# Phase 1 of a linear-attention kernel in another order, with part of the weight split moved from VectorE to GpSimd and ScalarE

## The reference

```python
def _linear_attention(x, wq, wk, wv, wo):
    q, k, v = (x @ wq), (x @ wk), (x @ wv)      # 16 heads of 16
    phi_q, phi_k = elu(q) + 1.0, elu(k) + 1.0
    kv = einsum('bshd,bshe->bhde', phi_k, v)
    z = sum(phi_k, axis=1)
    num = einsum('bshd,bhde->bshe', phi_q, kv)
    den = einsum('bshd,bhd->bsh', phi_q, z)[..., None] + 1e-06
    return (num / den).reshape(B, S, D) @ wo

y = layernorm(x)
y = y + _linear_attention(layernorm(y, ln1_g, ln1_b), wq, wk, wv, wo)
h = layernorm(y, ln2_g, ln2_b)
y = y + table[round(h @ w1 / 0.1)] @ w2          # table: gelu on a grid of 0.1
x = x + y
return x + einsum('bsk,nk->bsn', layernorm(x), CB) * (SCB / 127.0) + bias
```

## Time and profile before

| | |
|---|---|
| median of 3 runs | 593.51 us (592.5 to 594.23) |
| the profiled execution | 594.68 us |
| its span from first to last instruction | 592.9 us |
| busy share of the span | PE 93%, PEld 83%, DVE 79%, ACT 65%, POOL 57% |
| phase 1 | from the first chunk to about 181 us of the span |
| mean granted TensorE clock | 0.981 |

### The profile page before, as it was taken

The page is one execution under the profiler, slowest core; times in us unless marked ns, Lnnn a source line. Parts: engine busy times, 40 slices in busy tenths (PEclk is TensorE's granted clock), DMA queues, the critical chain, the costliest instruction groups (busy, mean ns, idle before and its releaser), DMA issues.

```text
span 592.9 us, 11272 instructions
## 1 busy us (share of the span) xinstructions
PE 549.6 (93%) x3610; PEld 490.9 (83%) x3610; DVE 466.2 (79%) x1067; ACT 384.8 (65%) x636; POOL 338.8 (57%) x328
## 2 busy tenths in 40 slices
PE   6899999999996889999999999999999999999893
PEld 6778788888885879889898898988988889898783
DVE  5889998688775487978879788788887888878645
ACT  2475664465565667858669586696865968758650
POOL 3431333324131367786776868768687676776662
PEclk9699998999999999999999999999999999999998
DMA  8321221121001010101101101011010110200001
GB/s 269 122 71 48 94 71 37 35 72 35 16 22 56 1 37 1 71 35 35 71 0 71 39 33 71 0 71 54 16 71 0 71 68 2 71 4 33 36 21 54
DMA packets 11419, 29.47 MB, mean 50 GB/s; under 512 B 2048, under 2 KB 4864, under 8 KB 11392
## 3 DMA queue, kind: packets, MB, share of 16 engines
q1 hardware_dynamic: 9472, 28.32, 13.4%
q10 hardware_dynamic: 1920, 0.79, 0.7%
HBM read 20.71 MB, written 8.39 MB: 49 GB/s over the span
## 4 chain that ended last, share of the span: by engine, by line
DVE 28%; PE 23%; issue 18%; ACT 15%; POOL 13%; DMA 2%; POOLq 1%; ACTq 0%; DVEq 0%; SPq 0%
PE psum L1002 22%; POOL f32r_arena L378 7%; DVE bn_stats L657 4%; ACT grid_index L580 3%; POOL f_arena L371 3%; DVE f_arena L793 3%; DVE f32r_arena L814 3%; ACT f32r_arena L593 3%; DVE f_arena L824 2%; DMA f_arena<-in_L_attn_x_dram 2%; DVE f32r_arena L810 2%; DVE bn_stats_b L657 2%; ACT f_arena L591 2%; ACT f32r_arena L528 2%; DVE f32r_arena L802 2%
## 5 line engine op out<-in xcount | busy, mean ns | idle before, releaser
L1002 PE MATMUL psum<-w_hi,f32r_arena 128*128 128x256 f32 x1280 | 176.9, 284 | 12.3 <-POOL f32r_arena L378 8.6
L1002 PEld LDWEIGHTS psum<-w_hi,f32r_arena 128*128 128x128 f32 x1280 | 164.0, 189 | 22.9 <-issue 16.9
L1002 PE MATMUL psum<-f32r_arena,w_hi 128*128 128x512 f32 x512 | 139.9, 403 | 1.5 <-issue 1.0
L378 POOL TENSOR_TENSOR f32r_arena<-f_arena,f32r_arena 128x512 fp32r<-128x512 f32 x64 | 85.9, 1342 | 94.6 <-ACT f32r_arena L593 54.1
L580 ACT ACTIVATE grid_index<-psum,w_bias_in_steps 128x512 int8<-128x512 f32 x128 | 86.7, 677 | 64.2 <-PE psum L1002 64.2
L1002 PEld LDWEIGHTS psum<-f32r_arena,w_hi 128*128 128x128 f32 x512 | 88.0, 188 | 19.9 <-ACT grid_index L580 5.8
L591 ACT ACTIVATE f_arena<-grid_index 128x512 f32<-128x512 int8 x128 | 80.9, 632 | 24.6 <-POOL f32r_arena L378 14.3
L593 ACT ACTIVATE f32r_arena<-grid_index 128x512 fp32r<-128x512 int8 x128 | 79.3, 619 | 0.0
L1002 PE MATMUL psum<-f32r_arena 128*128 128x256 f32 (+1 forms) x384 | 71.6, 336 | 2.0 <-DVE f32r_arena L696 2.0
L1002 PEld LDWEIGHTS psum<-f32r_arena 128*128 128x128 f32 x384 | 59.2, 195 | 8.4 <-issue 2.2
L802 DVE TENSOR_TENSOR f32r_arena<-f_arena,f32r_arena 128x512 fp32r<-128x512 f32 x64 | 63.2, 988 | 2.1 <-ACT f32r_arena L593 1.8
(11 more groups left out here) (116 smaller groups left out, 916.2 us busy)
## 6 DMA issues: line engine op xcount, KB each, us to landing
f_arena<-in_L_attn_x_dram SPq DMA_DIRECT2D x32, 512.0 KB, 3.3
out_dram<-f_arena SPq DMA_DIRECT2D x15, 512.0 KB, 2.7
f_arena<-in_L_attn_w_dram SPq DMA_DIRECT2D x2, 1024.0 KB, 12.6
out_dram<-f_arena SPq DMA_DIRECT2D x2, 256.0 KB, 3.3
phi_q<-in_L_attn_wk_dram ACTq DMA_DIRECT2D x1, 256.0 KB, 4.7
phi_q<-in_L_attn_wq_dram SPq DMA_DIRECT2D x1, 256.0 KB, 4.9
phi_q<-in_L_ffn_CB_dram SPq DMA_DIRECT2D x1, 256.0 KB, 7.0
phi_q<-in_L_attn_wo_dram SPq DMA_DIRECT2D x1, 256.0 KB, 7.5
```

What stands on the lines that cost most here:

```text
L378: nc.gpsimd.tensor_tensor(t_lo[m % SLOTS], tf[m % 2], t_hi[m % SLOTS].bitcast(F32), ALU.subtract).then_inc(s["t_lo_p"], 1)
L1002: return nc.tensor.matmul(out_, lhs, rhs, start=start, stop=stop, skip_group_check=True)
```

## The change

DVE makes the `bn_stats` in two halves around `phi_key` 0, takes `bn_aggr` behind `phi_key` 1, and then `high1`, `low1` and `phi_query`. PE makes both key pairs before `turn1`, and in chunk 8 the first `gather` comes before `project_bias`. ACT takes both K halves before `gain1`. The wide weights are split in 8 slices of 576 columns, one in each of the first 8 chunks: ACT copies a slice behind `q_relus`, POOL subtracts in the next chunk ahead of `power1`, and ACT takes the sum of absolute values in place of the maximum. In chunk 8 the test of wo moves behind `norm1`. The number of weight columns is the same.

```diff
-    SLICES = PAIRS // 2
+    SLICES = PER_SEQ
     SLICE = W2ND // SLICES
...
@@ gpsimd
+            def weight_rest(n, c):
+                g.wait_ge(s["w_hi_done"], n + 1)
+                g.wait_ge(s["n1_ready"], c + 2)
+                nc.gpsimd.tensor_tensor(w_lo[:, split_cols(n)], w_raw[:, split_cols(n)], w_hi[:, split_cols(n)].bitcast(F32),
+                                        ALU.subtract).then_inc(s["w_lo_done"], 1)
...
+                    if past(c, 1) and splits(c - 1):
+                        weight_rest(it * 2 + (p - 1), c)
                     if within(c + 2):
                         power1(c + 2, p)
...
@@ scalar
+            def rest_flag(n):
+                a.wait_ge(s["w_lo_done"], n + 1)
+                wait(a, s["w_flag"], n)
+                act(rest_size[:, :], w_lo[:, split_cols(n)].bitcast(F32), ACT.Abs,
+                    accum_out=flag_cols[:, bass.ds(n + 2, 1)]).then_inc(s["w_flag"], 1)
...
-                if splits(it):
-                    act(w_hi[:, bass.ds(it * SLICE, SLICE)], w_raw[:, bass.ds(it * SLICE, SLICE)], ACT.Copy).then_inc(s["w_hi_done"], 1)
...
                     k_pair(c, 0)
+                    k_pair(c, 1)
                     if within(c + 1):
                         gain1(c + 1)
...
-                    k_pair(c, 1)
                     if past(c, 1):
                         q_relus(c - 1)
+                    if splits(c):
+                        act(w_hi[:, split_cols(c)], w_raw[:, split_cols(c)], ACT.Copy).then_inc(s["w_hi_done"], 1)
+                    if past(c, 1) and splits(c - 1):
+                        rest_flag(it * 2 + (p - 1))
...
@@ vector
                     if within(c + 2):
-                        stats1(c + 2, p, it + 1)
+                        half_sums1(c + 2, p, it + 1, 0)
                     phi_key(c, 0)
-                    if p == 0 and splits(it):
...
-                        ve.tensor_tensor(w_lo[:, cols], w_raw[:, cols], w_hi[:, cols].bitcast(F32),
-                                         ALU.subtract).then_inc(s["w_lo_done"], 1)
-                    if p == 1 and splits(it):
...
-                        ve.tensor_reduce(flag_cols[:, at], w_lo[:, cols].bitcast(F32),
-                                         AX.X, ALU.max, apply_absolute_value=True).then_inc(s["w_flag"], 1)
+                    if within(c + 2):
+                        half_sums1(c + 2, p, it + 1, 1)
+                    phi_key(c, 1)
+                    if within(c + 2):
+                        mean_var(c + 2, bn, mv1[p], "bn1", "mv1_ready")
+                    if is_chunk(c, PER_SEQ + 1):
+                        flag_value(PP, 2, "flag2")
                     if within(c + 1):
                         high1(c + 1, 1 - p)
-                    phi_key(c, 1)
-                    if is_chunk(c, PER_SEQ + 1):
-                        flag_value(PP, 2, "flag2")
+                        low1(c + 1, 1 - p)
                     if past(c, 1):
                         phi_query(c - 1)
-                    if within(c + 1):
-                        low1(c + 1, 1 - p)
...
@@ tensor
                         key_pair(c, p, 0)
+                        key_pair(c, p, 1)
                         if within(c + 1):
                             turn1(c + 1, 1 - p)
...
-                        key_pair(c, p, 1)
+                        gather(c, p, 0)
                         if is_chunk(c, PER_SEQ):
                             pe.wait_ge(s["a1_ready"], c + 2)
                             project_bias(TP)
-                        gather(c, p, 0)
```

More of the change, by code:

```diff
@@ L125, in build @@
         k8 = sb("grid_index", [P, 2, CHUNK], I8)
+        rest_size = sb("weights_rest_size", [P, SLICE])
         h_bias = sb("w1_bias_in_steps", [P, MT])
@@ L216, in tm, with splits, split_cols @@
             return a.rearrange("p (j d) -> p j d", j=TT)
-        def splits(it):
-            return not isinstance(it, int) or it < SLICES
+        def splits(c):
+            return not isinstance(c, int) or c < SLICES
+        def split_cols(c):
+            return bass.ds(c * SLICE, SLICE)
         def half_tm(a, h):
@@ L427, in pair @@
                         power(0, u2, r2, mv2, "mv2_ready", "u2_ready", "pow2")
-            with g.Fori(0, PER_SEQ // 2) as it:
+            pair(0)
+            with g.Fori(1, PER_SEQ // 2) as it:
                 pair(it)
@@ L669, in stats1, with half_sums1 @@
                 stats(c, x1[p], bn, mv1[p], "bn1", "mv1_ready")
+            def half_sums1(c, p, turn, h):
+                if h == 0:
+                    v.wait_ge(x1_loaded[p], 16 * (turn + 1))
+                for j in (2 * h, 2 * h + 1):
+                    i = ve.bn_stats(bn[:, 6 * j:6 * j + 6], tm(x1[p])[:, j])
+                if h == 1:
+                    i.then_inc(s["bn1"], 1)
             def norm1(c, p):
@@ L892, in pair @@
                     if within(c + 2):
-                        stats1(c + 2, p, it + 1)
+                        half_sums1(c + 2, p, it + 1, 0)
                     phi_key(c, 0)
-                    if p == 0 and splits(it):
-                        cols = slice(it * SLICE, it * SLICE + SLICE) if isinstance(it, int) else bass.ds(it * SLICE, SLICE)
-                        v.wait_ge(s["w_hi_done"], it + 1)
-                        ve.tensor_tensor(w_lo[:, cols], w_raw[:, cols], w_hi[:, cols].bitcast(F32),
-                                         ALU.subtract).then_inc(s["w_lo_done"], 1)
-                    if p == 1 and splits(it):
-                        cols = slice(it * SLICE, it * SLICE + SLICE) if isinstance(it, int) else bass.ds(it * SLICE, SLICE)
-                        at = slice(it + 2, it + 3) if isinstance(it, int) else bass.ds(it + 2, 1)
-                        v.wait_ge(s["w_lo_done"], it + 1)
-                        ve.tensor_reduce(flag_cols[:, at], w_lo[:, cols].bitcast(F32),
-                                         AX.X, ALU.max, apply_absolute_value=True).then_inc(s["w_flag"], 1)
+                    if within(c + 2):
[5 more added lines that the diff above has]
+                        flag_value(PP, 2, "flag2")
                     if within(c + 1):
                         high1(c + 1, 1 - p)
-                    phi_key(c, 1)
-                    if is_chunk(c, PER_SEQ + 1):
-                        flag_value(PP, 2, "flag2")
+                        low1(c + 1, 1 - p)
                     if past(c, 1):
                         phi_query(c - 1)
-                    if within(c + 1):
-                        low1(c + 1, 1 - p)
[L915 to L919, removed]
-                        flag_column(2, SLICES + 1, 4 + SLICES)
                     if is_chunk(c, PER_SEQ + 1):
@@ L930, in pair @@
                         norm1(c + 2, p)
+                    if is_chunk(c, PER_SEQ):
+                        v.wait_ge(s["wo_lo_done"], KT)
+                        ve.tensor_reduce(flag_cols[:, 2 + SLICES:3 + SLICES], wo_lo[:, :].bitcast(F32), AX.X, ALU.max,
+                                         apply_absolute_value=True).then_inc(s["wo_flag"], 1)
+                        v.wait_ge(s["wo_flag"], 1)
+                        v.wait_ge(s["w_flag"], SLICES)
+                        flag_column(2, SLICES + 1, 4 + SLICES)
                     if is_chunk(c, PER_SEQ + 5):
```

2 lines of the change are left out of this document (1 added, 1 removed).

## The result

The change made the kernel slower: 598.5 us median of 4 runs (597.55 to 599.34) against 593.17 us, a ratio of 1.0095 with a 95% interval of 1.0071 to 1.0119. I had forecast 593.1 us, with a range from 587.4 to 596.6. The profiled execution took 597.55 us with a span of 595.7 us, 2.8 us more than before; its mean granted clock was 0.973, before the change 0.981.

The account below looks back on a forecast made before the run. Prediction: POOL's late power holds loop chunks at 9.20 us. Chunks 0 to 8 -1.6, chunk 9 -0.6, chunks 9 to 15 +2.6 gave 0.4 us gain off the 593.51 us median: 593.1 us, range 587.4 to 596.6.

Parts of the forecast that it names:

- start, to chunk 2: Chunk 0: the second gather no longer waits for `gain1`, a gain of 0.5 us.
- loop, chunks 2 to 7: Loop chunks: DVE's saved work returns as a 1.55 us wait for POOL's power; 9.20 us per chunk, no gain.
- chunk 8, until PE resumes: Chunk 8: PE resumes 1.6 us later, at 98.8, with chunk 0's gain of 0.5 us included.
- chunk 8, clock: Chunk 8: low clock stays at 6.83 us, costing 3.4 us as before; bound 1.7 us either way.
- chunk 9: Chunk 9: `flag_value` ahead of cast and `low1` makes the block matmuls wait about 0.6 us.
- chunks 10 to 15: Late chunks: 2.6 us gained of PE's 4.6 us of waits for `phi_key` in chunks 9 to 15; ends 0 and 4.6.
- Chunk 8's idle time: Chunk 8: bias matmuls come behind a gather and PE is idle for 2 to 3 us.
- The chain: Loop: from `norm1` through `turn1`, `gain1`, cast, `low1`, `phi_query`, power and shift to scaling, 9.20 us.
- The early power: Loop rival: cast 0.45 us or more after `bn_aggr`, chunk at 8.3 to 8.4 us, 587.7 us; chance 0.32.
- no slipping-in: Loop rival: POOL's L313 gets in only behind `phi_query`, 0.29 us more in nine chunks, 595.7 us; chance 0.12.
- the held port: Loop rival: the power gets in first and keeps the cast out, chain 10.1 us, 598.4 us; chance 0.02.
- table load: ACT rival: the sum of absolute values loads tables, costing 0 to 8 us, middle 597 us; chance 0.02.

Follow-up runs that it names:

- early_bias_first: Changed kernel with `bn_aggr` ahead of `phi_key` 1 and chunk 8's bias matmuls ahead of gather 0: 586.4 us, ratio 0.9868 to before.
- bias_first: Changed kernel with one step undone, chunk 8's bias matmuls ahead of the first gather again: 592.97 us, ratio 0.9988 to before.
- aggr_early: Changed kernel with `bn_aggr` moved ahead of `phi_key` 1: 588.26 us, ratio 0.9888 to before.
- bias_cut: Changed kernel with only 4 of chunk 8's 32 bias matmuls kept: 590.8 us, ratio 0.9953 to before.
- stats_first: Changed kernel with all four `bn_stats` and `bn_aggr` ahead of both `phi_key` again: 593.13 us, ratio 0.9983 to before.
- weights_only: Kernel before with only the weight work moved to POOL and ACT, every order kept: 592.27 us, ratio 0.9982 to before.
- early_bias_ahead: Changed kernel with `bn_aggr` ahead of `phi_key` 1 and the bias matmuls ahead of chunk 8's key pairs: 586.63 us, ratio 0.9868 to before.

## Why the prediction was wrong, and where it held

The terms of the sum, in us of gain, forecast and read from the two traces:

| term | forecast | measured |
|---|---|---|
| start, to chunk 2 | +0.5 | +2.03 |
| loop, chunks 2 to 7 | 0 | +0.25 |
| chunk 8, until PE resumes | -2.1 | -2.97 |
| chunk 8, clock | 0 (1.7 either way) | -3.93 |
| chunk 9 | -0.6 | -0.39 |
| chunks 10 to 15 | +2.6 | +2.25 |
| sum | +0.4 | -2.76 |

**The step that failed is the clock of chunk 8.** I kept the 6.83 us of the earlier trace rows and left half of that open. It became 17.07 us, and the term that stood at nothing cost 3.93 us. The price is borne out by the traces in which PE does the same matmuls, in one order or the other, from where it resumes to gather 0 of chunk 9: 15.31 us with 6.83 us of low clock (before), 15.33 with 6.83 (early_bias_first), 16.95 with 10.24 (bias_first), 18.56 with 13.65 (aggr_early) and 19.24 with 17.07 (changed, 15.06 of them behind the point where PE resumes).

I had read the earlier trace rows as a low clock behind the bias. By the earlier trace rows the bias runs from 97.20 to 102.64, so the clock fell at 98.93, within the bias; in the changed kernel it fell in the idle time, ahead of the bias. The prediction said itself that PE would be idle 2 to 3 us ahead of this place and that the bias matmuls would follow; the mistake was to take the row of before as the value for another sequence of work, and to bound it by that row's own length. The range was narrow by its own terms, too: the two bounds named for it, 1.7 and 2.6 us, give 597.4 us, not 596. The trace of before had two low stretches with different work in them: the bias, and the start, where PE worked with gaps and no bias:

```profile
13.60:23.84 10.24, 6.92 (x30) 5.97 (x29) 8.40 (x27) 6.13 (x10) 4.79 (x11) 0.50 0.68 209
```

A change that puts a gap and the bias next to each other could have been bounded by the sum of the two, 17.07 us, in place of half of one; 10.24 us more at half speed are up to 5.1 us. That the sum is just what was measured is luck: no run shows that such lengths add, and aggr_early, with gap and bias together, had 13.65 us. With the one step undone that brings gap and bias together, the time is 592.97 us. That this is within 0.2 us of the forecast is luck as well, since 10.24 us of low clock stay and PE resumes 1.99 us earlier.

**What the traces leave open.** The sums of the table differ by 3.2 us, the forecast and the median by 5.4. The profiled execution of before is 1.5 us above its median and that of the changed kernel 0.95 us below. That part of the loss lies in executions that were not profiled, and I can't place it. What is on record of them is their mean granted clock: 0.968 to 0.973 in the changed kernel's four, 0.973 to 0.987 in the 31 executions of the kernel before beside bias_first (median 0.981), and in both the longer executions have, on the whole, the lower clocks. That points at the clock, but not at a place in the kernel. Why the stretch of low clock differs in length between executions of one kernel stays open.

**The start** gave more than forecast. The second gather of chunk 0 no longer waits, as I said, but most of the 2.03 us come with the clock: it is low for 6.83 us in place of 10.24 us there. bias_cut is the changed kernel up to chunk 8; there the low stretch was 10.24 us, and `phi_key` 0 of chunk 2 comes at 39.95, which leaves a gain of 0.72 us, near the 0.5 forecast.

**Chunk 8's idle time** was 3.80 us, not 2 to 3, and the loss until PE resumes was 0.9 us larger than forecast. This term is the smaller miss.

**The loop held.** The chain gave 9.20 us; it is 9.10 to 9.20, with L705 waiting 1.53 us (1.55 forecast), L316, L317 and L322 at 0.43, 1.20 and 2.49 us (0.7, 1.2 and above 2.5 forecast). The early power did not come in this order: the cast is ahead of L316 by 0.28 us (49.97 and 50.25), where my sum gave 0.24; aggr_early shows its point, a cast 0.50 us behind `bn_aggr` (0.45 forecast), and its price, a chunk of 8.46 us against 8.3 to 8.4. The rivals of no slipping-in and of the held port did not happen. The page "SBUF — State Buffer" of the Trainium skill, section "Who interferes with whom", would have the second to issue wait for the first in either direction. With DVE first the rows agree: L316 behind the cast. With POOL first they don't: in stats_first the cast took its usual 0.69 us inside a power that ran from 57.86 to 60.00. In weights_only a cast from 50.52 to 51.21 stood in the middle of a power from 50.20 to 51.84, and both took their usual times; in stats_first the cast ran until 59.96, past the 59.50 at which a power of 1.64 us would have ended, and the power ended 0.04 us behind it.

**The rest held**: `weight_rest` took 1.42 us (1.34 to 1.51), hidden; `rest_flag` 0.69 us and a step of 0.20 us for the sum (0.73 to 1.6), and no table load stands beside it. The Trainium skill, page "ScalarE: Activation LUTs", section "Table sets: the hidden batching unit", lists abs among the functions of every set, and the trace agrees.

## What to carry to other kernels

When an operation moves, follow the consumers of its result on the other engines, too: `bn_aggr` moved by one operation decided 0.7 us per chunk, though neither DVE nor POOL had more to do. Treat a low clock as a result of the order of the work around it: here a gap on PE and a run of tiny matmuls went with 13.65 to 17.07 us of low clock together, and with 6.83 to 10.24 us apart, so a move that brings them together needs a bound well above what either cost before. Small PE work that stood in the gap (bias_first) cost 5.5 us less than the same work behind it.

## What the runs showed of the hardware

- The clock stayed at 1.2 GHz for 17.07 us although PE was busy for 15.06 of them; 32 matmuls of one column took 6.83 us of that (4.54 us in early_bias_ahead, 2.50 of them at full speed). With extra matmuls of no use in the gap the median was 6 us lower, though the one execution with a trace was not.
- A POOL operation that meets a row of DVE operations on SBUF gets in between two of them, one operation for each: 0.43, 1.20 and 2.49 us for work that took 0.19, 0.20 and 1.64 us in weights_only. A cast that stood in the middle of a power delayed neither.
- The same kernel differs by several us between executions (aggr_early from 586.32 to 592.77 us, with mean granted clocks of 0.981 and 0.969), so one profiled execution is no measure of a few us.
